# Attention block with routed experts on one core: the query factor sent through DRAM, and half of the heads with a separate maximum

## The reference

```python
qh = _lora_proj(_layernorm(x), Wq, ...)     # 16 heads of 16
scores = jnp.einsum('bqhd,bkhd->bhqk', qh * SCALE, kh) + attn_bias
p = jax.nn.softmax(scores, axis=-1)
out = jnp.einsum('bhqk,bkhd->bqhd', p, vh)
x = x + jnp.tanh(g_xattn[0]) * out
...
x = x + jnp.tanh(g_ffn[0]) * expert(_layernorm(x))   # one expert of 8 by the largest logit
```

## Time and profile before

| | |
|---|---|
| median of 3 runs | 1283.41 us (1283.16 to 1283.64) |
| the profiled execution | 1286.07 us, span 1284.2 us |
| granted TensorE clock | 0.991 of full speed |
| busy share of the span | PE 97%, PEld 83%, POOL 78%, DVE 78%, ACT 61% |
| DMA | 280.34 MB, mean 218 GB/s |

### The profile page before, as it was taken

The page is one execution under the profiler, slowest core; times in us unless marked ns, Lnnn a source line. Parts: engine busy times, 40 slices in busy tenths (PEclk is TensorE's granted clock), DMA queues, the critical chain, the costliest instruction groups (busy, mean ns, idle before and its releaser), DMA issues.

```text
span 1284.2 us, 45363 instructions
## 1 busy us (share of the span) xinstructions
PE 1250.6 (97%) x12696; PEld 1071.5 (83%) x12696; DVE 996.9 (78%) x5961; ACT 781.1 (61%) x1724; POOL 999.9 (78%) x1051
## 2 busy tenths in 40 slices
PE   8999999999999999999999999999998799999997
PEld 6888888888888888888888888887887678888886
DVE  6778888888888888888888888887897556555654
ACT  2767667677767676777676767776676333333332
POOL 3778889889888888888888888888888544554545
PEclk9999999999999999999999999999999899999999
DMA  7656666666666666666666666666666388988885
GB/s 261 221 192 219 215 203 208 207 210 213 201 207 217 212 202 213 209 213 201 209 221 206 210 206 219 203 201 198 204 201 217 120 251 275 283 278 274 284 268 181
DMA packets 119875, 280.34 MB, mean 218 GB/s; under 512 B 16356, under 2 KB 35302, under 8 KB 119680
## 3 DMA queue, kind: packets, MB, share of 16 engines
q1 hardware_dynamic: 106128, 243.55, 59.7%
q0 software_dynamic: 12624, 34.62, 6.9%
q10 hardware_dynamic: 1056, 1.39, 0.4%
HBM read 243.50 MB, written 36.91 MB: 218 GB/s over the span
## 4 chain that ended last, share of the span: by engine, by line
PE 90%; issue 3%; DVE 3%; DMA 1%; POOL 1%; another core or an unknown queue 1%; ACT 1%; POOLq 0%; DVEq 0%; ACTq 0%
PE bank L600 18%; PE bank L625 17%; PE bank L575 11%; PE bank L609 9%; PE bank L735 8%; PE bank L778 8%; PE bank L792 7%; PE bank L676 4%; PE bank L749 2%; PE bank L766 2%; DMA out<-og,ids 1%; PE bank L648 1%; PE bank L707 1%; DVE sc L1035 1%
## 5 line engine op out<-in xcount | busy, mean ns | idle before, releaser
L1035 DVE CUSTOM_DVE_ANT_0 sc<-bank,sc 128x128 f32<-128x128 f32 x2048 | 442.9, 286 | 121.6 <-PE bank L575 109.9
L462 POOL TENSOR_TENSOR sc<-sc,rowmax 128x1024 f32<-128x1024 f32 x256 | 480.3, 1900 | 21.0 <-DVE rowmax L1035 16.7
L876 ACT ACTIVATE PT<-bank 128x512 f32<-128x512 f32 x512 | 279.9, 603 | 2.5 <-PE bank L600 1.8
L600 PE MATMUL bank<-cst,sc 128*128 128x128 f32 x2048 | 272.6, 276 | 0.6 <-POOL sc L462 0.6
L600 PEld LDWEIGHTS bank<-cst,sc 128*128 128x128 f32 x2048 | 225.4, 140 | 26.6 <-issue 25.3
L534 POOL DMA_INDIRECT out<-og,ids x120 | 118.3, 986 | 120.4 <-issue 113.7
L519 POOL DMA_INDIRECT rows_dram<-x2n,slot_i x128 | 135.2, 1056 | 62.1 <-issue 55.8
L1035 DVE DVE_READ_ACCUMULATOR2_ANT rowmax<- 128x1 f32 x2048 | 170.1, 83 | 0.2 <-issue 0.2
L870 ACT COPY OT<-bank 128x512 f32<-128x512 f32 x128 | 75.0, 586 | 134.9 <-PE bank L609 134.9
L575 PE MATMUL bank<-KT,QT 32*128 32x256 f32 x2048 | 146.7, 400 | 3.4 <-ACT V L917 1.2
L609 PE MATMUL bank<-PT,V 128*32 128x128 f32 x4096 | 137.6, 275 | 0.6 <-ACT PT L876 0.6
(11 more groups left out here) (151 smaller groups left out, 1964.4 us busy)
## 6 DMA issues: line engine op xcount, KB each, us to landing
sc<-in_bias SPq DMA_DIRECT2D x256, 512.0 KB
w_sb<-in_w SPq DMA_DIRECT2D x69, 257.0 KB
CT<-in_w SPq DMA_DIRECT2D x69, 256.0 KB
xg<-rows_dram SPq DMA_DIRECT2D x63, 272.0 KB
x_sb<-in_x SPq DMA_DIRECT2D x128, 128.0 KB, 2.0
CT<-in_ctx_in SPq DMA_DIRECT2D x64, 256.0 KB, 4.7
XT<-in_x_turned SPq DMA_DIRECT2D x64, 256.0 KB, 2.7
rows_dram<-x2n,slot_i POOLq DMA_INDIRECT x128
```

Of the source, the lines that this page charges most:

```text
L462: nc.gpsimd.tensor_tensor(s, s, m, ALU.subtract).then_inc(sub_ok, 1)
L600: ins = nc.tensor.transpose(turn_bank(t, q)[:, P * h:P * h + P], sc[:, t.slot(4), o:o + P], ident)
L876: nc.scalar.activation(PT[:, t.slot(2), 512 * q:512 * q + 512], turn_bank(t, q)[:], ACT.Exp).then_inc(pt_ready, 1)
L1035: ins = nc.vector.tensor_tensor_reduce(out=s, in0=b_s[q][:, P * (h % 4):P * (h % 4) + P], in1=s, scale=1.0, scalar=LOWEST, op0=ALU.add, op ...
```

## The change

The two transposes on PE and the copy on ACT go. Instead, in every step, DVE transposes the factor column of one sequence in blocks of 32x32 (`turn_scale`, four steps ahead of the sequence's scores), ACT sends the four rows of 32 numbers to a DRAM tensor (`send_scale`, after the copy of V), waits for that to land, and issues a second transfer that reads them back to all 128 partitions (`spread_scale`, at the end of its step). RS is doubled, and the wait of the values' projection for the copy of RS goes with it.

In `add_bias` the first two groups (eight heads) stay as they are; for the last two groups there is one plain addition of 128x512 each, and after them one maximum over 128x1024 (`later_max`). POOL's second subtraction waits for this maximum.

```diff
+        rs_dram = nc.dram_tensor("rs_dram", (N, STRIPS, STRIP), F32, kind="Internal").ap()
...
-        RS = sb("RS", [P, 2 * P])
+        RS, rs_turned = sb("RS", [P, 2, 2 * P]), sb("rs_turned", [P, 2, STRIP])
...
             def subtract_max(t, h):
-                pool.wait_ge(s_used, t.n(4, 2 * h + 2))
+                if h == 0:
+                    pool.wait_ge(s_used, t.n(4, 2))
+                else:
+                    pool.wait_ge(max_ok, t.n(1, 1))
...
-                if qry and qry.slot(2) == 0:
-                    pe.wait_ge(rs_ok, qry.n(1, 2))
-                    if not cur and val.reached(1):
-                        pe.wait_ge(v_evac, val.n())
-                    for n in range(2):
-                        rs = ln[:, (qry.k + n - 7) % 8, 0, 0:1].broadcast_to([P, P])
-                        ins = nc.tensor.transpose(b_rs[:, P * n:P * n + P], rs, ident)
-                    ins.then_inc(rs_ready, 1)
...
-                    if qry and qry.slot(2) == 0:
-                        pe.wait_ge(rs_evac, qry.per(2, 1, 1))
-                    elif not cur and val.reached(1):
+                    if not cur and val.reached(1):
                         pe.wait_ge(v_evac, val.n())
...
+            def send_scale(t):
+                act.wait_ge(rs_turn, t.n(1, 1))
+                act.nop(nofuse=True)
+                act.dma_start(rs_dram[t.n()], rs_turned[0:P:STRIP, t.slot(2), :]).then_inc(rs_out, 16)
+
+            def spread_scale(t):
+                pair, tok = t.k // 2 % 2, P * t.slot(2)
+                act.wait_ge(rs_out, t.n(16, 16))
+                act.nop(nofuse=True)
+                act.dma_start(RS[:, pair, tok:tok + P], rs_dram[t.n()].rearrange("(a b) c -> a (b c)", a=1)
+                              .partition_broadcast(P)).then_inc(rs_in[pair], 16)
...
+                behind = seq(i, k, -4)
...
-                if qry and qry.slot(2) == 0:
-                    act.wait_ge(rs_ready, qry.per(2, 1, 1))
-                    nc.scalar.copy(RS[:], b_rs).then_inc(rs_evac, 1)
...
                     nc.scalar.copy(V[:, val.slot(8), :, 0:D],
                                    b_v.rearrange("p (h d) -> p h d", d=D)).then_inc(v_evac, 1)
+                if behind:
+                    send_scale(behind)
                 if old:
                     act.wait_ge(x2t_ready, old.n(1, 1))
...
                 if qry and qry.slot(2) == 0:
                     queries(qry)
+                if behind:
+                    spread_scale(behind)
...
                 dve.wait_ge(s_ready, t.n(4, q + 1))
-                dve.nop(nofuse=True)
+                if q < 2:
+                    dve.nop(nofuse=True)
+                if q >= 2:
+                    s = sc[:, t.slot(4), 512 * q:512 * q + 512]
+                    nc.vector.tensor_tensor(s, b_s[q][:], s, ALU.add).then_inc(s_used, 1)
+                    return
...
+            def later_max(t):
+                dve.wait_ge(s_used, t.n(4, 4))
+                nc.vector.tensor_reduce(rowmax[:, t.slot(2), 8:16],
+                                        sc[:, t.slot(4), 1024:2048].rearrange("p (h k) -> p h k", h=8),
+                                        AX.X, ALU.max).then_inc(max_ok, 1)
...
             def scale_queries(t):
                 pair = t.k // 2 % 2
-                dve.wait_ge(rs_evac, t.per(2, 1, 1))
+                dve.wait_ge(rs_in[pair], t.per(4, 32, 32))
                 for o in range(KC):
                     dve.wait_ge(q_ready, t.per(2, KC, o + 1))
-                    ins = nc.vector.tensor_tensor(QT[:, pair, o, :], b_s[o][:, 0:2 * P], RS[:], ALU.mult)
+                    ins = nc.vector.tensor_tensor(QT[:, pair, o, :], b_s[o][:, 0:2 * P], RS[:, pair, :], ALU.mult)
                 ins.then_inc(scaled_ok, 1)
+
+            def turn_scale(t):
+                dve.wait_ge(rs_ok, t.n(1, 1))
+                if t.reached(2):
+                    dve.wait_ge(rs_out, t.n(16, -16))
+                dve.nop(nofuse=True)
+                nc.vector.transpose(rs_turned[:, t.slot(2), :], ln[:, (t.k - 7) % 8, 0, 0:1].broadcast_to([P, STRIP])
+                                    ).then_inc(rs_turn, 1)
...
                     for q in range(4):
                         add_bias(cur, q)
+                    later_max(cur)
+                if behind:
+                    turn_scale(behind)
                 if here.reached(2) and (gate or done or grp):
                     dve.wait_ge(o_ready, here.n(1, -1))
```

More of the change, by code:

```diff
@@ L200, in flamingo_block @@
         b_x, b_o = bank[6], bank[7]
-        b_v, b_rs, b_x2 = b_x[:, 0:HID], b_x[:, HID:HID + 2 * P], b_s[3]
+        b_v, b_x2 = b_x[:, 0:HID], b_s[3]
         o_ps = b_o[:].rearrange("p (h c) -> p h c", c=CELL)
@@ L252, in flamingo_block @@
         xT_in = [sem(f"xT_in{i}") for i in range(2)]
-        rs_ready, rs_evac = sem("rs_ready"), sem("rs_evac")
+        rs_turn, rs_out, rs_in = sem("rs_turn"), sem("rs_out"), [sem(f"rs_in{i}") for i in range(2)]
         s_setc, scaled_ok = sem("s_setc"), sem("scaled_ok")
@@ L256, in flamingo_block @@
         q_ready, q_evac, k_ready, k_evac = sem("q_ready"), sem("q_evac"), sem("k_ready"), sem("k_evac")
-        s_ready, s_used, sub_ok = sem("s_ready"), sem("s_used"), sem("sub_ok")
+        s_ready, s_used, max_ok, sub_ok = sem("s_ready"), sem("s_used"), sem("max_ok"), sem("sub_ok")
         tr_ready, pt_ready = sem("tr_ready"), sem("pt_ready")
@@ L1090, in scale_queries @@
                 pair = t.k // 2 % 2
-                dve.wait_ge(rs_evac, t.per(2, 1, 1))
+                dve.wait_ge(rs_in[pair], t.per(4, 32, 32))
                 for o in range(KC):
                     dve.wait_ge(q_ready, t.per(2, KC, o + 1))
-                    ins = nc.vector.tensor_tensor(QT[:, pair, o, :], b_s[o][:, 0:2 * P], RS[:], ALU.mult)
+                    ins = nc.vector.tensor_tensor(QT[:, pair, o, :], b_s[o][:, 0:2 * P], RS[:, pair, :], ALU.mult)
                 ins.then_inc(scaled_ok, 1)
+            def turn_scale(t):
[5 more added lines that the diff above has]
+                                    ).then_inc(rs_turn, 1)
             def step(i, k):
                 cur, done, gate, ahead = seq(i, k, 0), seq(i, k, 2), seq(i, k, 4), seq(i, k, -5)
-                qry = seq(i, k, -2)
+                qry, behind = seq(i, k, -2), seq(i, k, -4)
                 grp, was_grp = seq(i, k, 5), seq(i, k, 6)
```

## The result

The changed kernel takes 1339.49 us (median of 4 runs, 1336.66 to 1340.86), the kernel before 1283.29 beside it: the ratio is 1.0436, interval 1.0417 to 1.0454. That is 56 us more where 31 were forecast, and 2.5 us above the range. The profiled execution took 1336.66 us, 50.6 more than that of before; its span is 1334.4 us, 50.2 more.

The account below looks back on a forecast made before the run. PE bounds the kernel, 97% busy, with DVE close behind. Growth of 0.89 us per four steps over 31 rounds, 27.6, plus 3 at the start gives 31 more: 1317 profiled, median 1314, range 1285 to 1337 (own case 1300 to 1326).

Parts of the forecast that it names:

- The even steps: Steps 0 and 2 of four on PE, with transposes and queries' projection; forecast 0.41 and 0.28 us longer, waiting for DVE's scaling.
- the last part of the prediction: Signs: odd scores released by DVE's scaling, even steps 7.7 to 8.0 us, new instructions 2.4 us; otherwise wrong.
- The other signs: Even steps of some 7.7 to 8.0 us, and DVE idle almost only before type 2's and 3's adds.
- Type 2: PE step with k modulo 4 equal to 2, 7.45 us before; forecast 0.28 us longer through DVE's scaling.
- type 0: PE step with k modulo 4 equal to 0, 7.55 us before; DVE picks experts first; forecast 0.41 us longer.
- the loop through DVE: Scores, DVE's adds and heads, queries' scaling, next scores; forecast to grow by 0.75 + 0.15 = 0.90 us.
- the 14.1 us on PE: Two transposes dropped from PE, 0.22 us per pair of sequences, 64 pairs; the most the change can take off PE.
- 0.1 us on PE in each odd step (0 to 0.4): Odd steps are types 1 and 3; ACT's send makes x2T some 0.3 us later, delaying the next scores.
- The sum for four steps: PE's growth per round of four steps: 0.28 + 0.41 + 2 x 0.1 = 0.89 us, over 31 rounds 27.6.
- 3 us once (2 to 6): Start of the kernel: the first pair's scaling waits for the second send and two landings of 2.0 us.
- The rivals: Faster, PE keeps the lead: 1272, chance 0.12; half the added time: 1291, 0.12; ACT waits for DRAM: 0.16.
- ACT waits for DRAM: Rival, chance 0.16: store over some 2.9 us delays ACT's output copy and PE; at 3.2 about 1335 us.

Follow-up runs that it names:

- with joined heads: The factor through DRAM as in the changed kernel, but all 16 heads joined as in the kernel before: 1338.68 us, ratio 1.0410 to the kernel before.
- SyncE's queue, joined: Changed kernel with all 16 heads joined as before and the factor's two transfers issued by SyncE instead of ScalarE: 1305.96 us, ratio 1.0167.
- an idle store at this place: Kernel before plus a 512-byte store nobody reads, issued by ScalarE between the copies of V and x2T: 1335.44 us with 4 rows, 1334.17 with 16.
- separate heads: Last eight heads by two additions and one maximum; alone on the kernel before, factor still by PE's transposes: 1303.29 us, ratio 1.0148.

## Why the prediction was right or wrong

**Right: the direction, and the prices on DVE.** Forecast were 0.68 us for an addition, 1.20 for the maximum and 0.15 for the turn; measured 0.683, 1.220 and 0.12 from the turn's start to the next. The even steps were to grow by 0.28 and 0.41 and grew by 0.18 and 0.24, and the scores after them are put down to the scaling, as the last part of the prediction asked for. That is luck: with joined heads, where the scaling ends 0.8 to 1.0 us ahead of the scores (medians), these steps are as long (7.79 and 7.62). The other signs held in part. Type 2's 7.63 lies below the 7.7 to 8.0, and DVE is idle ahead of the adds in types 0 and 1 too, 0.42 and 0.22 us beside 1.22 and 0.68 in types 2 and 3 (medians). In type 0 the loop through DVE is also shorter than assumed. The first add comes 1.27 after the scores (537.70 and 536.43) and not 1.47 or 1.73, for the pick's comparison takes 0.63 us now, where it took 1.50:

```profile
535.75 0.63 DVE L1084 TENSOR_TENSOR best<-L,lmax 128x32 f32<-128x32 f32 x1
...
537.70 0.29 DVE L1048 CUSTOM_DVE_ANT_0 sc<-bank,sc 128x128 f32<-128x128 f32 x1 [0.46 <-PE bank L579]
```

**Right, but of no use: the 14.1 us on PE.** They exist; type 2 falls from 7.45 to 7.23 where ScalarE is out of the way (SyncE's queue, joined). In the changed kernel PE waits them away, as forecast.

**Wrong: ScalarE's step.** The prediction said: "An issue on ACT took 0.34 and ran beside the copy before it, so x2T comes some 0.3 later: 0.1 us on PE in each odd step (0 to 0.4). In even steps the scaling covers it." Three things in it failed. The send's issue takes 0.55, not 0.34. In the rows above it starts 0.11 to 0.26 us after V's copy does, and x2T starts only 0.1 after its end, so the delay is 0.5 to 0.66. And of the 0.24 us between x2T's end and the scores only some 0.1 were room, for the scores still start 0.10 after that end when they wait for it: with an idle store at this place a delay of 0.48 cost 0.36 to 0.45. The odd steps grew by 0.40 to 0.52, up to five times the 0.1 that was taken, and beyond its upper end of 0.4. The even steps are not covered by the scaling: with joined heads, without DVE's longer work, they have the same length. The sum for four steps was 0.89 and is 1.30. For the 30 rounds from the eighth step on that makes 12 us of the miss.

**Wrong: the start.** "3 us once (2 to 6)" is 12.1. The chain was the right one (V, second send, two landings), but a landing of 2.0 us from the earlier trace rows is a median of the loop; among the first loads the stores took 5.6 us and the spread 6.1, and a later spread's wait held the output copy 3.9 us. This is another 9 us; together 21, where the profiled executions miss the sum by 20 (50.6 against 30.6). The medians miss by 25.5: the profiled run of the changed kernel lies 2.8 us under its median, that of the kernel before 2.7 above its own.

**Left out: DMA traffic.** "SP's and POOL's queues are not touched" is true of the queues, not of their transfers: a load like the spread cost 10 us alone, as its waits show by way of POOL's scatter. In the changed kernel POOL's wait for the scatter is only 8.7 us from 100 to 960 us, and the send and the start already account for the whole miss. So this term, put at nothing, is not why the forecast failed.

**The rivals.** None of the named mechanisms is the cause. "ACT waits for DRAM" gives nearly the time measured (1335; its own terms, 1314 + 64 x 0.3, give 1333). But ACT's instructions are held by the send's landing only twice, 9.7 us in all, both early. In the loop the spread mostly goes out 1.7 to 2.2 us after the send, about as assumed, and no copy behind it is held. A time that fits is no proof of its mechanism.

**What stands in the end.** The factor through DRAM costs what it does because of where its send stands: moved ahead of V, with joined heads, 1338.68 becomes 1301.21. Most of the 17 us that are left is the start (12.4 in the profiled run); the rest lies in the steps, where the transfers' traffic is the likely cause. The separate heads cost 18 us alone and 28.5 on top of a well-placed factor. In the changed kernel the two hide behind one another, which is why taking away either alone shows almost nothing or little: 1338.68 without the heads, 1329.74 without the bad place, 1301.21 without both.

## What to carry to other kernels

Cost a DMA issue as an instruction of its engine, with its own duration, and look at what is queued around it: here it cost nothing with work already queued ahead of it or in an idle stretch, and nearly its whole length in every step between two short copies of which the second releases another engine. The time between the end of an instruction and the start of what needs it is no slack unless a run has shown that a delay there is free; an idle copy put at the place measures it. And when two limits lie within 0.2 us of each other, undo both at once as well as each alone, for either one hides the other.

## What the runs showed of the hardware that was not expected

An issue on ScalarE's queue took 0.55 us for the send (512 bytes, 4 rows) and 0.33 to 0.39 for the spread (64 KB to 128 rows); a store of 16 rows still took 0.51, so the number of rows alone is not the reason.

The keys' activations run on while the same engine issues a DMA (518.02 to 518.55, beside a group that goes on to 518.83), but a copy that stands behind the issue starts only 0.1 us after its end (543.08 + 0.55, then 543.75). The Trainium skill, "DMA: Bandwidth & Descriptors", section "Issuing engines are not separate DMA queues", says that issuing from several engines saves only the sequencer's time for the issue, which it calls usually small beside the transfer. The runs agree with the first half: with joined heads, SyncE's queue for the same transfers was 33 us faster. Small it is, 0.55 us, and 128 times on the path.

A reduction of 1024 elements from SBUF took 1.22 us and a turn of 128x32 0.20. The same 512-byte store let its spread go after 1.7 us in the loop (median) and after 5.6 to 6.6 among the first loads.
